# A chunk's convolutions mixed tile by tile with the projection of the chunk in front, in one buffer whose layout alternates

## The chip, the cores and the metric

One core of a Trainium2 chip. The metric is the device time of one execution in microseconds, as the median of several runs.

## The reference

The input x is (128 batch, 128 time, 512 features), float32. Two blocks are added to it, one after the other. The first is a causal convolution along time with 128 taps for each feature, two projections, and a gated linear recurrence; the second is a tanh recurrence. Cut to what matters:

```python
# block 1: conv_w = cond[:, None, :], K = 128 taps, one filter for each feature
x_pad = jnp.pad(x, ((0, 0), (K - 1, 0), (0, 0)))
conv = conv_b + sum(x_pad[:, k:k + L, :] * conv_w[k, 0] for k in range(K))
proj = conv @ Wp + bp                          # 512 -> 128
B_t, C_t = softplus(proj[..., :64]), tanh(proj[..., 64:])
u = x @ Ws + bs                                # 512 -> 64
state = decay * state + dt * B_t * u_t         # over time, y_t = C_t * state
x = x + (y @ Wo + bo)
# block 2: 128 rows, 128 steps, h0 = cond
h = tanh(h @ Wh + x_t @ Wx + b)                # over time
x = x + h
```

## The kernel before

**First phase: convolution and projection.** The 512 features are four chunks (`KC` = 4) of 128. For each feature `d` the convolution over time is one matmul, `x_ring` (time x batch, time reversed) as stationary and `t_ring`, the Toeplitz matrix of the feature's taps, as moving operand: 128 batch rows by 128 times. The float32 matmul is carried out as two records in the profile. Four features (`PER_BANK`) fill a PSUM bank; that is a tile, and a chunk has 32 (`BANKS`). Both operands come from a ring of 8 slots, each of 8 features (`CH`), 896 KB in three transfers, that SP's queue issues when `conv_done` says that the slot has been used (`load_ring`). ScalarE copies even banks and VectorE odd banks into `conv`, laid out [batch, time, feature], so each copy writes runs of four elements 512 bytes apart.

`projection(c)` starts when the chunk is copied whole. Tile m of it takes four times: four transposes turn `conv[:, t]` (batch x feature) into feature x batch in a bank of `TURN`, ScalarE copies it with the convolution's bias added to one of four slots of `turned` (`copy_turned`), and one matmul with 512 columns multiplies by the chunk's `wp_now` (two records again). Its result is added by VectorE to `bc` (`add_proj`), the sum over chunks. TensorE issues the projection of tile m - 3 after the transposes of tile m (`LAG` = 3). So TensorE's order is convolution(0), projection(0), convolution(1), and so on, the first three chunks in a loop run by the engines (`Fori`), the fourth written out. The chunk's Wp (128 x 257, with the bias as last column) is loaded by SP when the projection before has ended, behind the eight ring loads that the chunk before lets out, and ahead of the next.

**In the last chunk's projection** ScalarE and VectorE also compute the softplus of the B rows by pairs of tiles (`soft_abs`, `soft_exp`, `soft_ln`, `soft_sum`), and GpSimd splits the weights and the first x of the second phase into high and low parts, once `conv_done` says that the convolutions are over and, for `x_lo`, `turn_done` that the transposes are.

**Second phase.** 32 groups of four time steps: the recurrence of block 1 on VectorE, one group ahead of the tanh recurrence of block 2 whose products are on TensorE. It isn't touched.

Of the kernel before, what the change touches and what calls it, by code (L numbers as in the profile page):

```python
# [12 lines left out]
TIME = 128  # L13
# [11 lines left out]
VECTORS = KC + 5  # L25
PAIRS = BANKS // 2
LAG = 3
# [10 lines left out]
def build(nc, x_rev, x_dtb, hankel, h0_t, vectors, Wp, Ws, Wo, Wx, Wh, b, out):  # L38
# [6 lines left out]
    with ctx:  # L45
# [7 lines left out]
        CONV, TURN, PROJ = bank[0:4], bank[4:6] + bank[0:2], bank[2:4] + bank[6:8]  # L53
# [11 lines left out]
        wo_f = turned[:, 3]  # L65
        vec = sb(ctx, "vec", [P, VECTORS])
        bo_c, bp_c, bs_c, logs = vec[:, 0:KC], vec[:, KC:KC + 2], vec[0:N, KC + 2:KC + 3], vec[:, KC + 3:KC + 5]
        rates = sb(ctx, "rates", [P, 4])
# [6 lines left out]
        with ExitStack() as first:  # L75


            t_ring = sb(first, "t_ring", [P, RING, CH // 2, TIME, 2])
            x_ring = sb(first, "x_ring", [P, RING, CH, BATCH])
            conv = sb(first, "conv", [P, TIME, P])  # L80
# [38 lines left out]
        def f(ap):  # L119
            return ap.bitcast(F32)  # L120

# [75 lines left out]
        def _(sp):  # L197
            def load_wp(c):
                rows = bass.ds(c * P, P)
                sp.dma_start(wp_now[:], Wp[rows, :]).then_inc(wp_loaded, DMA)  # L200

# [23 lines left out]
            for q in range(per_chunk - RING):  # L225
                sp.wait_ge(conv_done, BANKS * (KC - 1) + CH // PER_BANK * (q + 1))
                load_ring(per_chunk * (KC - 1) + q + RING, q % RING)
# [115 lines left out]
        def _(act):  # L343
# [7 lines left out]
            def copy_conv(c):  # L351
                with act.Fori(0, BANKS // 4) as i:
                    m = 4 * i
                    for k in (0, 2):

                        act.wait_ge(conv_done, BANKS * c + m + k + 1)
                        nc.scalar.copy(conv[:, :, bass.ds((m + k) * PER_BANK, PER_BANK)],
                                       CONV[k][:].rearrange("p (d l) -> p l d", d=PER_BANK)).then_inc(conv_copied_act, 1)

                act.wait_ge(wp_loaded, DMA * (c + 1))  # L360

            def copy_turned(c, m, k):

                act.wait_ge(turn_done, BANKS * c + m + k + 1)
                nc.scalar.activation(turned[:, k], TURN[k][:], ACT.Identity, bias=wp_now[:, 2 * P:2 * P + 1])\
                  .then_inc(turn_copied, 1)

            act.wait_ge(weights_ready, 2)
            with act.Fori(0, KC - 1) as c:
                copy_conv(c)  # L370
                with act.Fori(0, BANKS // 4) as i:
                    for k in range(4):
                        copy_turned(c, 4 * i, k)


            nc.scalar.preload_act_table_set("natural_log_exp_and_others")
            copy_conv(KC - 1)
# [25 lines left out]
            def pair(q, i, soft_too):  # L403

                m = 2 * q - (2 * i) % 4
                copy_turned(KC - 1, m, (2 * i) % 4)
                if soft_too:
                    soft_exp(q - 3, soft[(i - 3) % SOFT_SLOTS])
                copy_turned(KC - 1, m, (2 * i) % 4 + 1)
                if soft_too:  # L410
                    soft_ln(q - 3, soft[(i - 3) % SOFT_SLOTS])
                    soft_abs_odd(q - 2, soft[(i - 2) % SOFT_SLOTS])

            for q in range(3):
                pair(q, q, False)
            soft_abs_odd(0, soft[0])
            pair(3, 3, True)
            with act.Fori(1, PAIRS // 4) as j:
                for i in range(4):
                    pair(4 * j + i, i, True)  # L420
# [50 lines left out]
        def _(dve):  # L471
# [19 lines left out]
            def copy_conv(c):  # L491
                with dve.Fori(0, BANKS // 4) as i:
                    m = 4 * i
                    for k in (1, 3):
                        dve.wait_ge(conv_done, BANKS * c + m + k + 1)
                        nc.vector.tensor_copy(conv[:, :, bass.ds((m + k) * PER_BANK, PER_BANK)],
                                              CONV[k][:].rearrange("p (d l) -> p l d", d=PER_BANK))\
                          .then_inc(conv_copied_dve, 1)

            def add_proj(c, m, k):  # L500
                dve.wait_ge(proj_done, BANKS * c + m + k + 1)
                cols = bass.ds((m + k) * 512, 512)
                nc.vector.tensor_tensor(bc[:, cols], PROJ[k][:], bc[:, cols], ALU.add).then_inc(proj_added, 1)  # L503


            copy_conv(0)
            with dve.Fori(0, BANKS // 4) as i:
                for k in range(4):
                    dve.wait_ge(proj_done, 4 * i + k + 1)
                    nc.vector.tensor_scalar(bc[:, bass.ds((4 * i + k) * 512, 512)], PROJ[k][:],  # L510
                                            bp_c[:, k % 2:k % 2 + 1], None, ALU.add).then_inc(proj_added, 1)
            with dve.Fori(1, KC - 1) as c:
                copy_conv(c)
                with dve.Fori(0, BANKS // 4) as i:
                    for k in range(4):
                        add_proj(c, 4 * i, k)


            copy_conv(KC - 1)
# [15 lines left out]
            def pair(q, i, soft_too):  # L535

                for par in range(2):
                    add_proj(KC - 1, 2 * q - (2 * i) % 4, (2 * i) % 4 + par)
                    if par == 0:
                        soft_abs_even(q, soft[i])  # L540
                    if soft_too:
                        soft_sum(q - 2, par, soft[(i - 2) % SOFT_SLOTS])

            for q in range(4):
                pair(q, q, q >= 2)
            with dve.Fori(1, PAIRS // 4) as j:
                for i in range(4):
                    pair(4 * j + i, i, True)
# [88 lines left out]
        def _(pe):  # L637
            pe.wait_ge(ident_ready, 1)

            def convolution(c):  # L640

                for d in range(P):
                    slot, m = (d // CH) % RING, d // PER_BANK
                    if d % CH == 0:
                        pe.wait_ge(t_zero, slot + 1)
                        pe.wait_ge(ring_loaded[slot], LOAD * (P // CH // RING) * c + LOAD * (d // CH // RING + 1))
# [8 lines left out]
                    if d % PER_BANK == PER_BANK - 1:  # L658
                        mm.then_inc(conv_done, 1)
# [161 lines left out]
```

## Time and profile before

| | us |
|---|---|
| median of 3 runs | 1268.31 (1265.29 to 1274.13) |
| profiled execution, its own time | 1267.0 |
| its span | 1265.2 |
| TensorE busy (share of span) | 1186.3 (94%) |
| VectorE, ScalarE, GpSimd busy | 657.2, 504.7, 333.3 |
| granted TensorE clock, mean | 0.981 |

The span runs from the first to the last instruction of the profiled execution. In the rows PE is TensorE's matmuls, PEld its weight loads, DVE VectorE, ACT ScalarE, POOL GpSimd, SPq SyncE's queue. Matmuls overlap in the records, so the pace of a row of them is read from their starts or from the length of a group, and not from one record's duration.

### The profile page before, as it was taken

What the parts mean: (1) busy time and instruction counts of PE and PEld (TensorE: products, weight loads), DVE (VectorE), ACT (ScalarE), POOL (GpSimd) and SP (SyncE); (2) the same over time, 40 slices, a digit from 0 to 9 for tenths busy, and PEclk for the clock granted to TensorE, in tenths of its full rate; (3) what the DMA queues carried; (4) which work ended last, traced back from release to release, by engine and by line L of the source; (5) the groups of instructions that cost most, each with busy time, mean ns of one, the idle gap of its engine ahead of it and who ended that gap; (6) DMA issues with size and microseconds to landing.
All of it is one profiled execution on the core that took longest, in us unless ns stands there. A gap on an engine that the chain in (4) does not pass through costs nothing.

```text
span 1265.2 us, 17115 instructions
## 1 busy us (share of the span) xinstructions
PE 1186.3 (94%) x5888; PEld 949.2 (75%) x5888; DVE 657.2 (52%) x1022; ACT 504.7 (40%) x756; POOL 333.3 (26%) x179
## 2 busy tenths in 40 slices
PE   5589799898859999999999999999999999999997
PEld 4567758577427888888888888888888888888886
DVE  2135254443996555555554555555555555455553
ACT  1144352443674434344433444443434443334432
POOL 1000000000432443333343333344333344333330
PEclk9889999998889999999999999999999999999999
DMA  9993957938102223222223322222322222322201
GB/s 213 236 233 80 271 147 205 264 96 214 45 0 67 68 81 106 80 66 66 66 66 101 98 66 66 66 66 90 101 74 66 66 66 70 107 88 66 66 34 67
DMA packets 82485, 129.54 MB, mean 102 GB/s; under 512 B 4960, under 2 KB 40800, under 8 KB 82464
## 3 DMA queue, kind: packets, MB, share of 16 engines
q1 hardware_dynamic: 82464, 129.26, 37.1%
q8 instruction: 13, 0.21, 0.1%
q14 instruction: 8, 0.07, 0.0%
HBM read 95.69 MB, written 33.55 MB: 102 GB/s over the span
## 4 chain that ended last, share of the span: by engine, by line
PE 85%; SPq 5%; DVE 3%; DMA 3%; issue 2%; ACT 0%; POOL 0%; DVEq 0%; POOLq 0%; ACTq 0%
PE bank L725 9%; PE bank L733 9%; PE bank L734 9%; PE bank L737 9%; PE bank L719 9%; PE bank L718 9%; PE bank L677 7%; PE bank L656 5%; PE bank L761 4%; PE bank L669 4%; DMA x_ring<-x_rev 3%; SPq L204 3%; PE bank L708 2%; PE bank L700 2%; PE bank L694 2%
## 5 line engine op out<-in xcount | busy, mean ns | idle before, releaser
L324 POOL TENSOR_TENSOR x_lo<-x_f,x_hi 128x512 fp32r<-128x512 f32 x126 | 160.0, 1300 | 555.7 <-ACT x_hi L442 555.7
L453 ACT ACTIVATE h_f<-z_f 128x512 f32<-128x512 f32 x128 | 80.9, 632 | 346.5 <-DVE z_f L612 346.5
L616 DVE TENSOR_TENSOR hT_lo<-bank,hT_hi 128x512 fp32r<-128x512 f32 x128 | 88.6, 692 | 216.1 <-ACT hT_hi L457 216.1
L733 PE MATMUL bank<-wh_hi,hT_hi 128*128 128x512 f32 x512 | 200.4, 391 | 0.0
L734 PE MATMUL bank<-wh_lo,hT_hi 128*128 128x512 f32 x512 | 199.8, 390 | 0.0
L719 PE MATMUL bank<-wx_lo,x_hi 128*128 128x512 f32 x512 | 199.7, 390 | 0.0
L718 PE MATMUL bank<-wx_hi,x_hi 128*128 128x512 f32 x512 | 199.4, 389 | 0.1
L656 PE MATMUL bank<-t_ring,x_ring 128*128 128x128 f32 x1024 | 134.8, 291 | 46.2 <-DMA x_ring<-x_rev 36.9
L656 PEld LDWEIGHTS bank<-t_ring,x_ring 128*128 128x128 f32 x1024 | 128.6, 202 | 53.4 <-issue 40.7
L612 DVE TENSOR_TENSOR z_f<-bank,b_rows 128x512 f32<-128x512 f32 x128 | 88.5, 692 | 132.5 <-PE bank L737 128.7
L318 POOL TENSOR_TENSOR x_lo<-x_f,x_hi 128x2048 fp32r<-128x2048 f32 x32 | 147.6, 4614 | 21.9 <-PE bank L669 21.8
L725 PE MATMUL bank<-wx_hi,x_lo 128*128 128x512 f32 x512 | 144.7, 404 | 0.3 <-POOL x_lo L324 0.3
L677 PE MATMUL bank<-turned,wp_now 128*128 128x512 f32 x256 | 133.5, 611 | 11.0 <-DVE bc L503 10.2
L737 PE MATMUL bank<-wh_hi,hT_lo 128*128 128x512 f32 x512 | 137.0, 389 | 0.0
L733 PEld LDWEIGHTS bank<-wh_hi,hT_hi 128*128 128x128 f32 x512 | 96.1, 188 | 25.9 <-ACT hT_hi L457 6.1
L457 ACT CAST hT_hi<-bank 128x512 fp32r<-128x512 f32 x128 | 75.2, 587 | 94.6 <-PE bank L761 94.6
L718 PEld LDWEIGHTS bank<-wx_hi,x_hi 128*128 128x128 f32 x512 | 96.1, 188 | 20.8 <-ACT x_hi L442 0.9
L669 PEld LDWEIGHTS bank<-ident,conv 128*128 128x128 f32 x512 | 63.3, 141 | 64.4 <-issue 64.4
L737 PEld LDWEIGHTS bank<-wh_hi,hT_lo 128*128 128x128 f32 x512 | 96.1, 188 | 20.4
L719 PEld LDWEIGHTS bank<-wx_lo,x_hi 128*128 128x128 f32 x512 | 96.1, 188 | 19.8
L734 PEld LDWEIGHTS bank<-wh_lo,hT_hi 128*128 128x128 f32 x512 | 96.2, 188 | 19.4
L442 ACT CAST x_hi<-x_f 128x512 fp32r<-128x512 f32 x128 | 79.5, 621 | 76.8 <-DVE x_f L589 74.5
(67 smaller groups left out, 1417.1 us busy)
## 6 DMA issues: line engine op xcount, KB each, us to landing
x_ring<-x_rev SPq DMA_DIRECT2D x64, 512.0 KB, 12.4
x_f<-x_dtb SPq DMA_DIRECT2D x32, 1024.0 KB, 8.1
out<-x_f SPq DMA_DIRECT2D x31, 1024.0 KB, 5.4
t_ring<-hankel SPq DMA_DIRECT2D x64, 256.0 KB, 11.4
t_ring<-hankel SPq DMA_DIRECT2D x64, 128.0 KB, 10.8
w_f<-Wx SPq DMA_DIRECT2D x1, 1024.0 KB, 5.5
w_f<-Wh SPq DMA_DIRECT2D x1, 1024.0 KB, 5.1
out<-x_f SPq DMA_DIRECT2D x4, 256.0 KB, 2.3
```

Of the source, the lines that this page charges most:

```text
L318: nc.gpsimd.tensor_tensor(x_lo[:], x_f[:, par], f(x_hi[:]), ALU.subtract).then_inc(xlo_ready, 1)
L324: nc.gpsimd.tensor_tensor(x1_lo[:, c], x1_f[:, par, c], f(x1_hi[:, c]), ALU.subtract)\
L616: nc.vector.tensor_tensor(hT_lo[:], turned_h, f(hT_hi[:]), ALU.subtract).then_inc(htlo_ready, 1)
L656: mm = nc.tensor.matmul(CONV[m % 4][:, bass.ts(d % PER_BANK, TIME)], x_ring[:, slot, d % CH], t_ring[:, slot, d % CH // 2, :, d % 2], star ...
L669: mm = nc.tensor.transpose(TURN[m % 4][:, bass.ts(i, P)], conv[:, m * PER_BANK + i], ident[:])
L677: nc.tensor.matmul(PROJ[n % 4][:], wp_now[:, bass.ts(n % 2, P)], turned[:, n % 4], start=True, stop=True)\
L718: nc.tensor.matmul(z, x1_hi[:, k, s], wx_hi[:, k], start=(k == 0), stop=False)
L719: nc.tensor.matmul(z, x1_hi[:, k, s], wx_lo[:, k], start=False, stop=False)
L725: mm = nc.tensor.matmul(z, x1_lo[:, k, s], wx_hi[:, k], start=False, stop=stop and k == KC - 1)
L733: nc.tensor.matmul(z, hT_hi[:, k], wh_hi[:, k], start=False, stop=False)
L734: nc.tensor.matmul(z, hT_hi[:, k], wh_lo[:, k], start=False, stop=False)
L737: mm = nc.tensor.matmul(z, hT_lo[:, k], wh_hi[:, k], start=False, stop=stop and k == KC - 1)
```

## The change

TensorE's order becomes: the 32 tiles of chunk 0's convolutions; then, for chunks c = 0, 1, 2 and each tile m, the transposes of tile m of chunk c, the convolutions of tile m of chunk c + 1, and the projection of tile m - 1 of chunk c; then the transposes and projections of chunk 3 with `LAG` 2. The copy of tile m of chunk c + 1 goes into the room in `conv` that the transposes of tile m of chunk c have just read. For that the layout alternates: even chunks lie as [batch, time, feature], as before, with the copy written by single elements 512 bytes apart; odd chunks lie as [batch, feature, time], with the copy contiguous and each transpose reading its 128 elements 512 bytes apart. VectorE's copies wait for `turn_done` of the tile; ScalarE's stand behind `copy_turned` of it. While chunks mix, `CONV` has four banks, `TURN` and `PROJ` two each; in the last projection four each. `turned` has three slots. Wp is loaded once (128 x 4 x 192) on SP's queue, behind the first eight ring loads; the convolution's bias moves to `vec`. All loops of the first phase are written out, and SP's ring loads depend on `conv_done` alone.

```diff
-VECTORS = KC + 5
+VECTORS = 2 * KC + 5
+WP = 3 * N
+SLOTS = 3
-LAG = 3
+LAG = 2
...
-        CONV, TURN, PROJ = bank[0:4], bank[4:6] + bank[0:2], bank[2:4] + bank[6:8]
+        CONV = bank[0:4]
+        TURN, PROJ = bank[4:6] + bank[0:2], bank[6:8] + bank[2:4]
...
-        wp_now = sb(ctx, "wp_now", [P, 2 * P + 1])
-        turned = sb(ctx, "turned", [P, 4, 512])
+        wp = sb(ctx, "wp", [P, KC, WP])
+        turned = sb(ctx, "turned", [P, SLOTS, 512])
...
+        def conv_room(c, m):
+            if c % 2:
+                return conv[:, bass.ts(m, PER_BANK)]
+            return conv[:, :, bass.ts(m, PER_BANK)].rearrange("p l d -> p d l")
+        def conv_at(c, t):
+            return conv[:, :, t] if c % 2 else conv[:, t]
+        def turn_bank(c, m):
+            return TURN[m % 4] if c == KC - 1 else TURN[m % 2]
+        def proj_bank(c, m):
+            return PROJ[m % 4] if c == KC - 1 else PROJ[m % 2]
+        def turned_slot(c, m):
+            return turned[:, (BANKS * c + m) % SLOTS]
...
@@ SP @@
-            load_wp(0)
-            per_chunk = P // CH
-            with sp.Fori(0, KC - 1) as c:
-                for q in range(per_chunk):
-                    sp.wait_ge(conv_done, BANKS * c + CH // PER_BANK * (q + 1))
-                    load_ring(per_chunk * c + q + RING, q % RING)
-                    if q == per_chunk - 1:
-                        sp.wait_ge(proj_done, BANKS * (c + 1))
-                        load_wp(c + 1)
...
+            sp.dma_start(wp[:], Wp.rearrange("(c p) n -> p c n", p=P)).then_inc(wp_loaded, DMA)
+            for n in range(RING, D // CH):
+                sp.wait_ge(conv_done, CH // PER_BANK * (n - RING + 1))
+                load_ring(n, n % RING)
@@ ScalarE @@
+            def copy_conv(c, m):
+                act.wait_ge(conv_done, BANKS * c + m + 1)
+                nc.scalar.copy(conv_room(c, m), CONV[m % 4][:].rearrange("p (d l) -> p d l", d=PER_BANK))\
+                  .then_inc(conv_copied_act, 1)
...
+            for m in range(0, BANKS, 2):
+                copy_conv(0, m)
+            for c in range(KC - 1):
+                for m in range(BANKS):
+                    copy_turned(c, m)
+                    if m % 2 == 0:
+                        copy_conv(c + 1, m)
...
@@ VectorE @@
+            def copy_conv(c, m):
+                dve.wait_ge(conv_done, BANKS * c + m + 1)
+                if c > 0:
+                    dve.wait_ge(turn_done, BANKS * (c - 1) + m + 1)
+                nc.vector.tensor_copy(conv_room(c, m), CONV[m % 4][:].rearrange("p (d l) -> p d l", d=PER_BANK))\
+                  .then_inc(conv_copied_dve, 1)
...
+            for m in range(1, BANKS, 2):
+                copy_conv(0, m)
+            for c in range(KC - 1):
+                for m in range(BANKS):
+                    if m % 2:
+                        copy_conv(c + 1, m)
+                    if m > 0:
+                        add_proj(c, m - 1)
+                add_proj(c, BANKS - 1)
@@ TensorE @@
+            def turn(c, m):
+                if m == 0:
+                    pe.wait_ge(conv_copied_act, BANKS // 2 * (c + 1))
+                    pe.wait_ge(conv_copied_dve, BANKS // 2 * (c + 1))
+                for i in range(PER_BANK):
+                    mm = nc.tensor.transpose(turn_bank(c, m)[:, bass.ts(i, P)], conv_at(c, m * PER_BANK + i), ident[:])
+                mm.then_inc(turn_done, 1)
+            def project(c, n):
+                pe.wait_ge(turn_copied, BANKS * c + n + 1)
+                freed = n - 3 if c == KC - 1 and n >= 2 else n - 1
+                wait(pe, proj_added, BANKS * c + freed)
+                nc.tensor.matmul(proj_bank(c, n)[:], wp[:, c, n % 2 * N:n % 2 * N + P], turned_slot(c, n), start=True, stop=True)\
+                  .then_inc(proj_done, 1)
+            for m in range(BANKS):
+                convolution(0, m)
+            pe.wait_ge(wp_loaded, DMA)
+            for c in range(KC - 1):
+                for m in range(BANKS):
+                    turn(c, m)
+                    convolution(c + 1, m)
+                    if m > 0:
+                        project(c, m - 1)
+                project(c, BANKS - 1)
+            for m in range(BANKS + LAG):
+                if m < BANKS:
+                    turn(KC - 1, m)
+                if m >= LAG:
+                    project(KC - 1, m - LAG)
```

## Rows read from the trace of the kernel before

**Rows 1.** Windows by stage: PE, PEld, DVE, ACT, POOL busy; PEclk, DMA share, GB/s.

```profile
8.00:75.00 67.00, 41.80 (x256) 38.28 (x256) 12.55 (x22) 9.69 (x18) 2.95 (x4) 0.87 1.09 235
75.00:117.00 42.00, 41.85 (x195) 25.06 (x196) 23.32 (x33) 21.67 (x32) 0.00 (x0) 1.00 0.62 132
117.00:153.00 36.00, 29.99 (x256) 29.03 (x254) 11.51 (x17) 9.38 (x16) 0.00 (x0) 1.00 0.98 243
...
271.00:309.00 38.00, 32.37 (x255) 31.14 (x253) 11.51 (x17) 9.38 (x16) 0.00 (x0) 0.91 0.85 197
...
382.00:1265.20 883.20, 876.44 (x4088) 718.59 (x4088) 473.04 (x764) 348.56 (x508) 301.78 (x157) 1.00 0.23 75
```

**Rows 2.** Chain that ended last: start us, us, what.

```profile
74.20 0.95 issue
75.14 1.94 PE bank L669 x16
...
308.39 0.95 issue
309.33 1.94 PE bank L669 x16
```

**Rows 3.** Timeline of TensorE in the convolutions: start us, us, what.

```profile
58.61 2.08 PE L656 MATMUL bank<-t_ring,x_ring 128*128 128x128 f32 x16 [1.90 <-DMA x_ring<-x_rev]
62.53 2.08 PE L656 MATMUL bank<-t_ring,x_ring 128*128 128x128 f32 x16 [1.85 <-DMA x_ring<-x_rev]
...
116.69 21.99 PE L656 MATMUL bank<-t_ring,x_ring 128*128 128x128 f32 x192
139.91 2.08 PE L656 MATMUL bank<-t_ring,x_ring 128*128 128x128 f32 x16 [1.23 <-DMA x_ring<-x_rev]
...
295.04 2.65 PE L656 MATMUL bank<-t_ring,x_ring 128*128 128x128 f32 x16 [2.18 <-issue]
299.33 3.75 PE L656 MATMUL bank<-t_ring,x_ring 128*128 128x128 f32 x16 [1.63 <-issue]
```

**Rows 4.** Timeline of one tile of chunk 0's projection.

```profile
79.08 0.60 PE L669 MATMUL bank<-ident,conv 128*128 128x128 f32 x4
...
79.52 1.02 PE L677 MATMUL bank<-turned,wp_now 128*128 128x512 f32 x2
...
80.38 0.60 PE L669 MATMUL bank<-ident,conv 128*128 128x128 f32 x4
80.38 0.36 PEld L669 LDWEIGHTS bank<-ident,conv 128*128 128x128 f32 x3 [0.29 <-issue]
```

**Rows 5.** DMA issues: KB each, median us from issue to landing.

```profile
x_ring<-x_rev SPq DMA_DIRECT2D x64, 512.0 KB, 12.4
...
wp_now<-Wp SPq DMA_DIRECT2D x4, 128.5 KB, 2.1
```

**Rows 6.** Groups of instructions by line, 0 to 440 us: busy, mean ns.

```profile
L365 ACT ACTIVATE turned<-bank,wp_now 128x512 f32<-128x512 f32 x128 | 86.6, 687 | 59.1 <-PE bank L669 58.7
...
L503 DVE TENSOR_TENSOR bc<-bank,bc 128x512 f32 (+1 forms) x96 | 66.1, 689 | 45.9 <-PE bank L677 45.5
L669 PEld LDWEIGHTS bank<-ident,conv 128*128 128x128 f32 x512 | 63.3, 141 | 64.4 <-issue 64.4
L496 DVE COPY conv<-bank 128x512 f32 x64 | 44.1, 691 | 121.8 <-PE bank L656 121.8
...
L357 ACT COPY conv<-bank 128x512 f32 x64 | 37.4, 586 | 135.1 <-PE bank L656 130.0 <-POOL wo_lo L279 5.1
```

**Rows 7.** Timeline of chunk 3's projection: VectorE and GpSimd.

```profile
342.16 0.69 DVE L503 TENSOR_TENSOR bc<-bank,bc 128x512 f32 x1
...
345.25 0.69 DVE L503 TENSOR_TENSOR bc<-bank,bc 128x512 f32 x1
...
358.65 4.51 POOL L318 TENSOR_TENSOR x_lo<-x_f,x_hi 128x2048 fp32r<-128x2048 f32 x1 [21.82 <-PE bank L669]
358.71 4.99 DVE L532 SCALAR_TENSOR_TENSOR bc<-bc,x_f 64x512 f32 x1
```

More of the change, by code:

```diff
@@ L79, in build @@
             x_ring = sb(first, "x_ring", [P, RING, CH, BATCH])
-            conv = sb(first, "conv", [P, TIME, P])
+            conv = sb(first, "conv", [P, P, P])
         wx_hi = sb(ctx, "wx_hi", [P, KC, D], F32R)
@@ L349, in _, with copy_turned @@
             nc.scalar.activation(rates[:, 2:4], rates_e[:], ACT.Ln, bias=1.0).then_inc(rate_act, 1)
[L351 to L365, printed above, removed]
+            def copy_conv(c, m):
+                act.wait_ge(conv_done, BANKS * c + m + 1)
+                nc.scalar.copy(conv_room(c, m), CONV[m % 4][:].rearrange("p (d l) -> p d l", d=PER_BANK))\
+                  .then_inc(conv_copied_act, 1)
+            def copy_turned(c, m):
+                act.wait_ge(turn_done, BANKS * c + m + 1)
+                nc.scalar.activation(turned_slot(c, m), turn_bank(c, m)[:], ACT.Identity, bias=conv_b[:, c:c + 1])\
                   .then_inc(turn_copied, 1)
+            act.wait_ge(vec_loaded, DMA)
             act.wait_ge(weights_ready, 2)
[L369 to L373, printed above, removed]
+            for m in range(0, BANKS, 2):
[5 more added lines that the diff above has]
+                        copy_conv(c + 1, m)
             nc.scalar.preload_act_table_set("natural_log_exp_and_others")
-            copy_conv(KC - 1)
             def u_copy(g):
@@ L401, in soft_ln @@
                 nc.scalar.activation(slot, slot, ACT.Ln, bias=1.0).then_inc(ln_ready, 1)
[L403 to L420, printed above, removed]
+            for q in range(PAIRS):
+                copy_turned(KC - 1, 2 * q)
+                if q > 2:
+                    soft_exp(q - 3, soft[(q - 3) % SOFT_SLOTS])
+                copy_turned(KC - 1, 2 * q + 1)
+                if q > 2:
+                    soft_ln(q - 3, soft[(q - 3) % SOFT_SLOTS])
+                if q > 1:
+                    soft_abs_odd(q - 2, soft[(q - 2) % SOFT_SLOTS])
             for q in range(PAIRS - 3, PAIRS):
@@ L489, in _ @@
             decay = rates[N:P, 1:2]
[L491 to L511, printed above, removed]
@@ L533, in soft_sum @@
                   .then_inc(b_ready, 1)
-            def pair(q, i, soft_too):
+            for q in range(PAIRS):
                 for par in range(2):
-                    add_proj(KC - 1, 2 * q - (2 * i) % 4, (2 * i) % 4 + par)
+                    add_proj(KC - 1, 2 * q + par)
                     if par == 0:
[L540 to L548, printed above, removed]
+                        soft_abs_even(q, soft[q % SOFT_SLOTS])
+                    if q > 1:
+                        soft_sum(q - 2, par, soft[(q - 2) % SOFT_SLOTS])
             def u_to_v(g, par):
@@ L680, in _ @@
-            with pe.Fori(0, KC - 1) as c:
-                convolution(c)
-                projection(c)
-                pe.wait_ge(proj_added, BANKS * (c + 1) - 2)
-            convolution(KC - 1)
-            projection(KC - 1)
+                mm.then_inc(conv_done, 1)
+            def turn(c, m):
[5 more added lines that the diff above has]
+                mm.then_inc(turn_done, 1)
```

58 lines of the change are left out of this document (20 added, 38 removed).

## The prediction

> **What bounds the kernel now.** I read the busy time by stage first [rows 1]. Chunk 0's convolutions (8 to 75 us) are bound by the loads: TensorE works 41.8 of 67 us while the DMA share is 1.09, all 16 queues' engines full. In each projection stage (75 to 117 us stands for three) it is the other way: TensorE is busy 41.85 of 42 us, and the DMA engines move 132 GB/s at a share of 0.62, since no more can be loaded than the ring's eight slots hold. Then the convolutions of the next chunk (117 to 153 us) find eight ready slots and sixteen to eat, and TensorE is at 29.99 of 36 us with the DMA share back at 0.98. So TensorE and the DMA engines take turns being idle. From 382 us on TensorE is busy 99% at a clock of 1.00; nothing of that recurrence is edited, and I take it as a fixed tail.
>
> Second, the chain of waits gives the borders [rows 2]: the first transpose of chunk 0 starts at 75.14 us, that of chunk 3 at 309.33. Before each lies 0.95 us in which the engine waited for nothing shown; it is the copy of the last bank (0.69 us on VectorE) that `projection` waits for. Third, the timeline of TensorE inside the convolutions [rows 3]: 192 records run in one piece (21.99 us), then pieces of 16 records (eight values of `d`, one ring slot) come singly, each released by a load. That is a used-up ring. Where the loads alone set the pace it is 62.53 - 58.61 = 3.92 us a slot in chunk 0, and at its slowest late in chunk 3, 299.33 - 295.04 = 4.29 us (named "issue", but it is the same rhythm at the same place, the thirteenth slot).
>
> **The change, part by part.** (1) *TensorE's work of the three mixed chunks.* It is the same work as before, so I price it at full pace. One tile of the projection stage repeats every 80.38 - 79.08 = 1.30 us [rows 4]: four transposes (79.08 to 79.52, 0.44 us) and two records of projection (0.86 us), with no gap. Over a stage, 41.7 us for 32 tiles (the stage's window shows 41.85 busy) is 1.303 us. The convolutions of one tile are eight records; the unbroken piece gives 21.99 us for 192, less 0.16 us of the last record's modelled drain (it lasts 0.27 us where the pace is 0.11), so 0.114 us a record and 0.91 us a tile. A mixed tile is therefore 1.30 + 0.91 = 2.21 us, and 3 x 32 of them are 212 us. Before, the same stretch took 309.33 - 75.14 = 234.2 us [rows 2]. The difference is 22.2 us. As a cross-check, it is 3 x 0.95 us of copy tails plus what the three convolution stages are longer than 29.1 us each; of 36 us in the window of chunk 1 TensorE idled 6, and chunk 3 lost more, to a clock of 0.91 as well as to waiting [rows 1].
>
> (2) *The ring.* Loads now run through the projections. A slot is eaten every two tiles, 4.42 us, against 3.92 us to fill one under full load and 4.29 us at the slowest [rows 3], so the ring gains on TensorE and the wait goes. The margin is thin at the start: chunk 0 ends with an empty ring, its last slots each being waited for, and a hiccup there shows. From the landing time of 12.4 us [rows 5] a late slot costs a part of one slot's time; I take 1 us, between 0 and 4.3 us (one whole slot at the slowest pace).
>
> (3) *Waits that the mixing adds,* all in tile m. `turn(m)` feeds the copy to `turned`, 0.69 us on ScalarE [rows 6], while TensorE has 0.91 us of convolutions and `project(m-1)` needs only the copy of the tile before, an age of 2.2 us. `project(m-1)` also needs `add_proj(m-3)`, which VectorE can begin when `project(m-3)` ends, over 3 us earlier. VectorE does per two tiles one conv copy and two adds, 3 x 0.69 = 2.07 us, ScalarE two copies to `turned` and one conv copy, 2 x 0.69 + 0.59 = 1.97 us, both of 4.42 us. VectorE's new wait on `turn_done` is met before `conv_done` of the same m, since TensorE does them in that order. ScalarE's copy of `conv(c+1, m)` blocks `copy_turned(m+1)` behind it, but that one's transposes come a full `project` later. The copy tail between chunks (0.95 us) now lies under two projections, 1.72 us. Cost 0, up to 0.05 us a tile (5 us) if the switches between three kinds of work leave bubbles that the present switches between two don't.
>
> (4) *Wp in one load.* It goes to SP's queue at the same place, behind the first eight slots and ahead of the ninth, and is 384 KB in place of 128.5 KB. Chunk 0 is bound by loads, so the 256 KB more count: at 235 GB/s [rows 1] 1.1 us. The small load takes 2.1 us to land [rows 5], so 0.5 to 3 us. The three later Wp loads, which stood in front of ring loads, go; they were hidden.
>
> (5) *The layout that alternates.* Even chunks are now copied by elements written 512 bytes apart, odd ones contiguously; the transposes of odd chunks read their weights 512 bytes apart. Before, copies wrote runs of four elements 512 bytes apart, and took 0.69 us on VectorE, the same as the contiguous add, and read their bank with that stride too [rows 6]. No row has single elements written or weights read so. For the copies I take no change (a gain is excluded, since they already take what a contiguous add of that size takes); doubled, VectorE would need 2.8 us of 4.42 and they would still be hidden. A transpose lasts 0.44 / 4 = 0.11 us, with the next weight load just under it (three loads in 0.36 us [rows 4]), so nothing hides a slower load. I take 0 here, since the bank-side stride cost nothing; the other value is a rival below.
>
> (6) *The last projection.* It is bound by VectorE: from one add of a pair to that of the next pair is 345.25 - 342.16 = 3.09 us [rows 7], against 2.6 us of TensorE for two tiles. LAG 2 in place of 3 lets the first projection start one tile's transposes earlier, 0.44 us, and takes a tile from the lead; in the steady state a projection waits for an add four back either way, and the copy needed is one pair old. `turned` with three slots is refilled only after TensorE has passed that projection. I take -0.3 us, between -1 and +3. GpSimd's splits that hold VectorE (4.99 us beside 4.51 us at 358.7 us [rows 7]) hang on the end of all convolutions and transposes, so they move along with the stage. Loops written out instead of run by the engines' counters change instruction supply; the stretch of chunk 0 runs written-out code at the loads' pace and the turn of the loop shows no gap after 116.69 us [rows 3], so 0.
>
> Sum: -22.2 + 1.0 + 1.1 - 0.3 = -20.4 us. The profiled execution took 1267.0 us (span 1265.2 and 1.8 around it), which becomes 1246.6. The median of the runs is 1.3 us above the profiled one: 1248 us. What is late next is TensorE itself through the mixed chunks, VectorE in the last projection.
>
> **A rule against the change.** The rows show strides without a price on VectorE's copies, and nothing on TensorE's weight side [rows 6]. The Trainium skill, SBUF — State Buffer, section Specifications (TRN2), says that SBUF is read by lines of 16 bytes and needs at least two hits on a line for full bandwidth. By that rule the strided weight loads of chunks 1 and 3 would slow down and the sum would be that of rival A or B; the old copies, with four elements to a line, don't contradict it.
>
> **The rivals.** *A: strided weight loads take twice their time.* A transpose then has 0.22 us; three of four loads are exposed (the first lies under a projection), 0.33 us a tile. Chunk 1: 32 x 0.33 = 10.6 us. Chunk 3: the tile becomes 1.63 us against VectorE's 1.55, 32 x 0.08 = 2.6 us. The gain of 20.4 shrinks to 7.2: 1261 us. For it: single elements in a line, and the pace of loads has no slack. Against: VectorE and ScalarE read and write at this stride at one element a cycle already [rows 6].
>
> *B, the slower side: strided weight loads take four times theirs.* Then 0.44 us each, 0.99 us more a tile: chunk 1 32 us, chunk 3 32 x (1.30 + 0.99 - 1.55) = 24 us, together 56 - 20.4 = 35 us slower, 1304 us. It costs more than the change gives from about 2.4 times on (1.4 x 0.11 x 3 = 0.46 us a tile, 15 us in chunk 1 and 7 us in chunk 3). No row shows such a price, and none excludes it.
>
> *C: the loads don't keep up.* If a slot took 4.9 us in the mix (the engines' own traffic beside it, 25% over chunk 0's 3.92), 48 slots would cost 0.48 us each, 23 us: the change only moves the wait, 1271 us. Against: the fill is 0.5 us faster than the use, and in chunk 1 the loads ran at 243 GB/s beside a busy TensorE [rows 1], where the mix asks for 0.92 MB in 4.42 us, 208 GB/s.
>
> *D: the mix leaves bubbles*, 0.05 us a tile and the ring starting empty: 1248 + 5 + 3 = 1256 us, just inside 1%.
>
> **How the numbers follow.** The forecast, the strides free and the ring ahead, 0.62; A 0.14; B 0.07; C 0.06; D 0.11. A measurement of this kernel tells no change from one within about 1%, 12.7 us. Faster by more is the forecast alone with part of D, 0.66; within 1% is A, C and the rest of D, 0.25; slower is B and the worst of C, 0.09. The forecast's own range is 1242 to 1254 (its bounds: 0 to 4.3 us for the ring, 0.5 to 3 for Wp, the last stage -1 to 3, and the runs before spread 1265.3 to 1274.1). To hold 8 in 10 it must take in D and A: 1241 to 1262.
>
> **What the profile would show.** In the mixed stretch TensorE busy at 99% with clock 1.00, a tile each 2.21 us, and DMA share about 0.85 throughout. The first transpose of chunk 3 near 288 us. No waits of the convolutions for `x_ring` after chunk 0. The last stage still 3.09 us a pair. If A or B holds, weight loads of transposes in chunks 1 and 3 last longer than the 141 ns of today's [rows 6] and those of chunks 0 and 2 don't; if C holds, waits for `x_ring` return every second tile; in D idle shows as small pieces between kinds of work. Wrong by a lot it would be if transposes read at a stride are slow, or if ScalarE's or VectorE's written strides push a copy beyond the 2.21 us of its tile.

## The result and the profile after

The changed kernel takes 1238.99 us (median of 4 runs, 1233.53 to 1241.46) against 1266.8 us before; the ratio on record is 0.9752, 95% interval 0.9711 to 0.9793 (the quotient of the two medians alone is 0.978). That is 27.8 us less by the medians, and 28.7 by the profiled executions (spans 1265.2 and 1236.5). The forecast was 1248 with a range down to 1241: right in direction, too small by 9 us.

Busy time by stage of the changed kernel, as [rows 1]: PE, PEld, DVE, ACT, POOL, then clock, DMA share and GB/s. The lines are chunk 0's convolutions, the three mixed chunks, and the fixed tail.

```profile
8.00:63.90 55.90, 35.85 (x254) 33.42 (x252) 17.87 (x22) 16.89 (x18) 2.95 (x4) 0.94 1.09 277
64.00:135.60 71.60, 71.02 (x448) 53.78 (x448) 34.20 (x47) 31.28 (x48) 0.00 (x0) 1.00 1.09 241
135.70:209.90 74.20, 74.20 (x449) 59.85 (x448) 35.91 (x49) 38.20 (x48) 0.00 (x0) 1.00 0.88 229
210.00:280.50 70.50, 70.50 (x449) 53.76 (x448) 33.09 (x48) 32.56 (x49) 0.00 (x0) 1.00 0.41 119
...
353.00:1236.50 883.50, 877.09 (x4088) 719.50 (x4088) 472.88 (x763) 348.57 (x508) 301.93 (x157) 1.00 0.24 75
```

The mix is what was forecast: TensorE is busy 71.02 of 71.6, 74.20 of 74.2 and 70.50 of 70.5 us, at a clock of 1.00. In the second chunk TensorE is as busy as in the others and the stage is 3.6 us longer: it does the same work more slowly. And chunk 0 is over at 63.9 us, with 277 GB/s where [rows 1] had 235.

The timeline of TensorE at the end of chunk 0, as [rows 3], and into the mix:

```profile
53.91 2.06 PE L639 MATMUL bank<-t_ring,x_ring 128*128 128x128 f32 x16 [1.34 <-issue]
57.30 2.05 PE L639 MATMUL bank<-t_ring,x_ring 128*128 128x128 f32 x16 [1.34 <-issue]
60.63 2.06 PE L639 MATMUL bank<-t_ring,x_ring 128*128 128x128 f32 x16 [1.28 <-issue]
63.89 0.63 PE L649 MATMUL bank<-ident,conv 128*128 128x128 f32 x4 [1.20 <-DVE conv L490]
64.82 1.18 PE L639 MATMUL bank<-t_ring,x_ring 128*128 128x128 f32 x8 [0.31 <-DMA x_ring<-x_rev]
...
68.92 1.18 PE L639 MATMUL bank<-t_ring,x_ring 128*128 128x128 f32 x8 [0.28 <-DMA x_ring<-x_rev]
...
75.21 0.60 PE L649 MATMUL bank<-ident,conv 128*128 128x128 f32 x4
...
77.41 0.60 PE L649 MATMUL bank<-ident,conv 128*128 128x128 f32 x4
```

A slot now comes every 3.4 us (53.91, 57.30, 60.63), not every 3.92 [rows 3]. The first transpose is at 63.89 us, not 75.14. Two ring waits in the mix (0.31 and 0.28 us) and then none.

The borders of the mixed chunks, where two projections follow each other (timeline of TensorE):

```profile
133.93 1.88 PE L657 MATMUL bank<-turned,wp 128*128 128x512 f32 x4
135.65 0.71 PE L649 MATMUL bank<-ident,conv 128*128 128x128 f32 x4
...
139.47 0.71 PE L649 MATMUL bank<-ident,conv 128*128 128x128 f32 x4
...
141.79 0.72 PE L649 MATMUL bank<-ident,conv 128*128 128x128 f32 x4
...
208.23 1.88 PE L657 MATMUL bank<-turned,wp 128*128 128x512 f32 x4
209.94 0.60 PE L649 MATMUL bank<-ident,conv 128*128 128x128 f32 x4
...
278.84 1.88 PE L657 MATMUL bank<-turned,wp 128*128 128x512 f32 x4
280.56 1.89 PE L649 MATMUL bank<-ident,conv 128*128 128x128 f32 x12
```

| stage | before, us | after, us | difference | forecast |
|---|---|---|---|---|
| to the first transpose | 75.14 | 63.89 | -11.25 | +1.1 |
| to chunk 3's first transpose | 234.19 | 280.56 - 63.89 = 216.67 | -17.5 | -21.2 |
| to the first `wo_product` (at 382.16 and 352.98) | 72.83 | 72.42 | -0.4 | -0.3 |
| rest | 883.04 | 883.52 | +0.5 | 0 |

The mixed stretch is 71.76 us (to 135.65), 74.29 (to 209.94) and 70.62 us. Thirty-two tiles of 2.21 us are 70.7, so the third is the sum of the forecast exactly, the first has 1.1 us of ring waits and start, and the second is 3.6 us over.

The kernel before differs much more between two profiles than the changed one. In a second profile of it (e9 below) the stretch from the first transpose to chunk 3's is 314.36 - 73.49 = 240.9 us, not 234.2; in a second profile of the changed kernel (e8) it is 276.92 - 61.37 = 215.6, not 216.7. So the second row of the table is -17.5 us in this pair of profiles and -25.3 in the other.

### The profile page after: what moved, and what is told of

It is laid out like the page before. It is cut to its first block, busy times and chain, and to the rows that moved or that the text cites. A ratio compares the mean times of both kernels' runs of the same rounds, so it can differ in the third digit from the quotient of the medians.

```text
span 1236.5 us, 15777 instructions
## 1 busy us (share of the span) xinstructions
PE 1184.0 (96%) x5888; PEld 956.6 (77%) x5888; DVE 665.2 (54%) x1022; ACT 520.5 (42%) x756; POOL 334.1 (27%) x179
## 4 chain that ended last, share of the span: by engine, by line
PE 90%; DVE 4%; DMA 2%; ACT 1%; SPq 1%; issue 1%; POOL 1%; POOLq 0%; DVEq 0%; ACTq 0%
PE bank L713 10%; PE bank L721 9%; PE bank L722 9%; PE bank L707 9%; PE bank L706 9%; PE bank L725 9%; PE bank L639 8%; PE bank L657 7%; PE bank L749 5%; PE bank L649 4%; PE bank L696 2%; PE bank L697 2%; PE bank L688 2%; PE bank L682 2%; DVE x_f L516 1%; DMA x_ring<-x_rev 1%
## 5 line engine op out<-in xcount | busy, mean ns | idle before, releaser
L639 PE MATMUL bank<-t_ring,x_ring 128*128 128x128 f32 x1024 | 140.4, 282 | 26.3 <-issue 14.3
L657 PE MATMUL bank<-turned,wp 128*128 128x512 f32 x256 | 133.7, 606 | 9.4 <-DVE bc L500 8.7
L369 ACT ACTIVATE turned<-bank,vec 128x512 f32<-128x512 f32 x128 | 87.9, 688 | 107.4 <-PE bank L649 107.1
L649 PEld LDWEIGHTS bank<-ident,conv 128*128 128x128 f32 x512 | 79.1, 190 | 62.3 <-issue 62.3
L452 ACT CAST hT_hi<-bank 128x512 fp32r<-128x512 f32 x128 | 75.1, 587 | 94.7 <-PE bank L749 94.7
```

The costliest lines, as they stand in the source:

```text
L639: mm = nc.tensor.matmul(CONV[m % 4][:, bass.ts(d % PER_BANK, TIME)], x_ring[:, slot, d % CH], t_ring[:, slot, d % CH // 2, :, d % 2], star ...
L649: mm = nc.tensor.transpose(turn_bank(c, m)[:, bass.ts(i, P)], conv_at(c, m * PER_BANK + i), ident[:])
L657: nc.tensor.matmul(proj_bank(c, n)[:], wp[:, c, n % 2 * N:n % 2 * N + P], turned_slot(c, n), start=True, stop=True)\
```

## The experiments

Chunk 0 has sixteen ring loads; I call them slot 0 to slot 15. In all experiments the "pace" is the time from TensorE's start on slot 11 to its start on slot 15, divided by four, and "first transpose" stands for the end of chunk 0. In the timeline of TensorE of the kernel before, slots 8, 11 and 15:

```profile
42.75 2.97 PE L656 MATMUL bank<-t_ring,x_ring 128*128 128x128 f32 x16 [4.01 <-DMA x_ring<-x_rev]
...
54.63 2.08 PE L656 MATMUL bank<-t_ring,x_ring 128*128 128x128 f32 x16 [1.76 <-DMA x_ring<-x_rev]
...
70.42 3.77 PE L656 MATMUL bank<-t_ring,x_ring 128*128 128x128 f32 x16 [1.05 <-DMA x_ring<-x_rev]
```

That is a pace of (70.42 - 54.63) / 4 = 3.95 us. The last slot's records took 3.77 us here, at a granted clock of 0.50 (1.2 GHz) from 70.42 to 74.20 us, and 2.06 us in the changed kernel: 1.7 of the 11.25 us are this, and not the loads.

Besides the mixing, two things differ that bear on the loads of chunk 0. `wp_now` (1028 bytes a partition, rounded up) and `turned` changed size, so all that is allocated after them moved: `t_ring` starts at byte 98080 of the partition before (32 above a multiple of 256) and at 98048 (a multiple of 256) after, `x_ring` the same. And SP's ring loads are written out. (The loops of the other engines are written out too, and Wp is one load; e6, e7 and e10 bear on these.)

**e1: the ring on the boundary, nothing else.** Two small tiles become one, which moves everything behind 32 bytes down.

```diff
-        rates = sb(ctx, "rates", [P, 4])
-        rates_e = sb(ctx, "rates_e", [P, 2])
+        rates_both = sb(ctx, "rates_both", [P, 6])
+        rates, rates_e = rates_both[:, 0:4], rates_both[:, 4:6]
...
```

> The kernel before with the ring, and all that lies behind it in SBUF, 32 bytes lower, on a multiple of 256 bytes as the change happens to put it; nothing else. Theory 'placement' (loads into rows off that boundary are slower): a ring slot fills in 3.4 us instead of 3.9, the first transpose starts near 64 us instead of 75, the convolution stages of chunks 1 to 3 shrink towards 30 us each, in all 15 to 24 us less: 1243 to 1252. Theories 'written-out loads' and 'Wp': no change, 1267.

1258.3 us, ratio 0.9885 (0.9819 to 0.9951). Slots 11 and 15 of chunk 0 in its timeline:

```profile
51.22 2.08 PE L656 MATMUL bank<-t_ring,x_ring 128*128 128x128 f32 x16 [1.14 <-DMA x_ring<-x_rev]
...
65.15 2.08 PE L656 MATMUL bank<-t_ring,x_ring 128*128 128x128 f32 x16 [1.45 <-DMA x_ring<-x_rev]
```

The pace is 3.48 us, the first transpose at 68.18. The later convolution stages didn't shrink: from the first transpose to chunk 3's it takes 301.05 - 68.18 = 232.9 us, before 234.2. So the placement speeds up the loads of chunk 0, and the first transpose comes 7 us sooner than in the first profile of the kernel before and 5.3 sooner than in the second; that it also shortens the other three stages was expected, and the profile doesn't show it. From slot 8 (41.01 us) to slot 15 it takes 24.1 us instead of 27.7.

**e2: the changed kernel, off the boundary.**

```diff
+        ring_shift = sb(ctx, "ring_shift", [P, 8])
```

> The changed kernel with 32 bytes of nothing ahead of the ring, so that it lies as before the change, off the multiple of 256 bytes. Theory 'placement': chunk 0 takes 11 us longer again, the slots of the mix are filled in 3.9 us and still in time for 4.4, so 1239 + 11 = 1250, which is about the forecast. Theories 'written-out loads' and 'Wp': 1239.

1242.49 us, ratio 0.9778 (0.9714 to 0.9842).

```profile
48.77 2.06 PE L641 MATMUL bank<-t_ring,x_ring 128*128 128x128 f32 x16 [1.63 <-issue]
...
62.81 2.05 PE L641 MATMUL bank<-t_ring,x_ring 128*128 128x128 f32 x16 [1.31 <-issue]
```

Pace 3.51 us, first transpose 66.06 against 63.89. The placement costs here, but 2 to 5 us (against 63.89 and the 61.37 of e8) and not 11: it isn't the whole. The time is 1242.5 and not the 1250 expected.

**e3: the loads written out, nothing else.**

```diff
-            with sp.Fori(0, KC - 1) as c:
+            for c in range(KC - 1):
```

> The kernel before with only SP's loop of ring loads written out, each with its own Wp as before. Theory 'written-out loads' (registers and the loop slow SP's issue): chunk 0 ends 11 us sooner, 1256 or less. Theory 'placement': the gaps between issues shrink but the queue is full anyway, 1267, first transpose at 75 us.

1266.3 us, ratio 0.9955 (0.9909 to 1.0002), first transpose 67.66, pace 3.73 us. The profile shows a gain in chunk 0, the times one that is just inside the noise. Neither theory alone was right. The gain isn't one of pace: from slot 8 (37.13 us) to slot 15 it takes 27.5 us, before 27.7. Slot 8 starts 5.6 us sooner, and the last slot runs at full clock, 1.7 us. The stretch from the first transpose to chunk 3's is 305.20 - 67.66 = 237.5 us, longer than the 234.2 of before, which eats 3.3 us of the gain.

**e4: strided weights in all chunks of the kernel before.**

```diff
-                        nc.scalar.copy(conv[:, :, bass.ds((m + k) * PER_BANK, PER_BANK)],
-                                       CONV[k][:].rearrange("p (d l) -> p l d", d=PER_BANK))
+                        nc.scalar.copy(conv[:, bass.ds((m + k) * PER_BANK, PER_BANK)],
+                                       CONV[k][:].rearrange("p (d l) -> p d l", d=PER_BANK))
...
-    nc.tensor.transpose(TURN[m % 4][:, bass.ts(i, P)], conv[:, m * PER_BANK + i], ident[:])
+    nc.tensor.transpose(TURN[m % 4][:, bass.ts(i, P)], conv[:, :, m * PER_BANK + i], ident[:])
```

(VectorE's copy alike.)

> The kernel before with the layout of odd chunks in all four: copies contiguous, every transpose reads its weights 512 bytes apart. If strided weight loads cost the 0.11 us a tile seen in the changed kernel's chunk 1 and nothing hides it: chunks 0 to 2 each 3.6 us longer, chunk 3 (bound by VectorE) not, +11 us: 1278. If the longer tile of chunk 1 came from something else in the mix (the copies' slow writes beside it): 1267, tiles of 1.30 us.

1283.82 us, ratio 1.0113 (1.0066 to 1.016). One tile in its timeline, beside [rows 4], and its groups by line, beside [rows 6]:

```profile
90.37 0.71 PE L669 MATMUL bank<-ident,conv 128*128 128x128 f32 x4
90.37 0.52 PEld L669 LDWEIGHTS bank<-ident,conv 128*128 128x128 f32 x3 [0.21 <-issue]
...
90.92 1.02 PE L677 MATMUL bank<-turned,wp_now 128*128 128x512 f32 x2
...
91.78 0.71 PE L669 MATMUL bank<-ident,conv 128*128 128x128 f32 x4
```

```profile
L669 PEld LDWEIGHTS bank<-ident,conv 128*128 128x128 f32 x512 | 92.8, 242 | 55.2 <-issue 55.2
...
L496 DVE COPY conv<-bank 128x512 f32 x64 | 44.2, 691 | 123.8 <-PE bank L656 123.8
...
L357 ACT COPY conv<-bank 128x512 f32 x64 | 37.4, 586 | 138.0 <-PE bank L656 132.9 <-POOL wo_lo L279 5.1
```

A tile repeats every 91.78 - 90.37 = 1.41 us instead of 1.30; three weight loads take 0.52 us instead of 0.36, and one 242 ns on average instead of 141, while the contiguous copies keep their 691 and 586 ns. The three projection stages are 45.5 us each instead of 41.7, 11.4 us together. From chunk 3's first transpose to the end it takes 1280.0 - 323.37 = 956.6 us, before 955.9: there VectorE hides it. What was expected of the stages held; the time, by the ratio 14 us longer, is some 3 us more than the 11 expected.

**e5: both side effects, no mixing.** The edits of e1 and e3 together.

> The kernel before with both of the changed kernel's side effects and no mixing: the ring on a multiple of 256 bytes, and SP's ring loads written out. If the two explain chunk 0 between them, the first transpose is at 64 to 65 us as in the changed kernel, and the time is about 1254 to 1256; what then still separates it from the changed kernel, some 16 us, is the mixing. If the mixing or the single Wp load speeds up chunk 0, the first transpose stays at 67 us or later.

1256.22 us, ratio 0.9896 (0.9863 to 0.993).

```profile
47.04 2.08 PE L656 MATMUL bank<-t_ring,x_ring 128*128 128x128 f32 x16 [0.86 <-DMA x_ring<-x_rev]
...
60.09 2.08 PE L656 MATMUL bank<-t_ring,x_ring 128*128 128x128 f32 x16 [1.13 <-DMA x_ring<-x_rev]
```

Pace 3.26 us, first transpose at 63.11, as in the changed kernel. From there to chunk 3's first transpose it is 297.13 - 63.11 = 234.0 us, as before (234.2). So without any mixing these two give the whole gain of chunk 0 and nothing else, and the mixing gives 234.0 - 216.7 = 17.3 us on top.

**e7: the mixing alone.** The changed kernel with e2's 32 bytes and SP's loop of before.

```diff
-            for n in range(RING, D // CH):
-                sp.wait_ge(conv_done, CH // PER_BANK * (n - RING + 1))
-                load_ring(n, n % RING)
+            with sp.Fori(0, KC - 1) as c:
+                for q in range(per_chunk):
+                    sp.wait_ge(conv_done, BANKS * c + CH // PER_BANK * (q + 1))
+                    load_ring(per_chunk * c + q + RING, q % RING)
+            for q in range(per_chunk - RING):
+                sp.wait_ge(conv_done, BANKS * (KC - 1) + CH // PER_BANK * (q + 1))
+                load_ring(per_chunk * (KC - 1) + q + RING, q % RING)
```

> The changed kernel with both side effects undone: 32 bytes ahead of the ring, and SP's loads in the loop of before. The mixing alone. If the forecast's sum was right but for these two, the first transpose is at 75 us or a little later, the mix takes 215 us, and the time is 1250, about 19 us under the kernel before. If the mixing itself is worth more than forecast: 1240.

1245.4 us (1242.15 to 1250.1), ratio 0.9809 (0.9761 to 0.9857), which on 1268.3 is 1244 (1238 to 1250); the forecast of 1248 lies in it. Pace 3.62 us. But the first transpose was expected at 75 us or a little later, and is at 68.37. Slot 8 begins at 38.05 us, where the kernel before has 42.75 and 42.62, though the ring and the loop are the same. So undoing the two side effects gives back only part of chunk 0: 5 to 7 us of its gain remain, and no run says by what. The mixed stretch is 284.51 - 68.37 = 216.1 us. By the profiles' spans the kernel is 24.7 us shorter than before, 6.8 of them in chunk 0 and 18.1 in the stretch: that its time agrees with the forecast is in part luck, since the forecast had chunk 0 longer and the mix worth more.

**e6: Wp later.** The one Wp load goes behind ring load 16 instead of 7 (counted from 0).

> The changed kernel with Wp's one load issued behind ring load 16 and not behind the eighth. If it takes its bytes' share of chunk 0 (384 KB at the 277 GB/s there, 1.4 us), the first transpose comes 1.4 us sooner and the time falls by about 1 us, within the noise of the times but not of the profile. If small rows of 768 bytes cost more: 2 to 3 us. If the queue hides it: nothing.

1240.13 us, ratio 0.9767 (0.9721 to 0.9812), pace 3.39 us.

```profile
61.10 2.05 PE L640 MATMUL bank<-t_ring,x_ring 128*128 128x128 f32 x16 [1.25 <-issue]
66.09 0.66 PE L650 MATMUL bank<-ident,conv 128*128 128x128 f32 x4 [2.94 <-DMA wp<-Wp]
```

The first transpose is later than with Wp early (63.89 and 61.37 in two profiles), because it now waits for Wp itself: the load was moved so far back that TensorE stands idle for 2.94 us before the mix, where the changed kernel has 1.20. What the loads of chunk 0 gain is therefore read from slot 15, at 61.10 us with Wp behind its loads, against 60.63 and 58.12 us with Wp ahead of them. No gain of the size expected; Wp's price in chunk 0 is below what one profile can tell, and may be nothing.

**e8 and e9: the two kernels again,** for how far profiles of one kernel differ.

> The changed kernel itself, on the chip and beside the runs of these three, for a second profile: how far do the stages differ between two profiles of one kernel. Expected 1239, first transpose within 1 us of 63.9, mixed stages of 71.8, 74.3 and 70.6 us within 0.5.

1238.07 us, ratio 0.9744 (0.9697 to 0.9791). First transpose 61.37, 2.5 us sooner and not within 1 us, pace 3.24 us.

```profile
61.37 0.63 PE L649 MATMUL bank<-ident,conv 128*128 128x128 f32 x4 [1.20 <-DVE conv L490]
...
276.92 1.89 PE L649 MATMUL bank<-ident,conv 128*128 128x128 f32 x12
```

The mixed stages, with borders at 132.00 and 206.31 us, are 70.6, 74.3 and 70.6 us: the last two as in the first profile, the first 1.1 us shorter, as no ring wait is left in it.

> The kernel before itself, for a second profile of it. So far three kernels with the loads in SP's loop and TensorE's, ScalarE's and VectorE's loops too begin slot 8 at 41.0 to 43.7 us, and the rest at 35.4 to 38.1. If that is the kernel and not the execution: slot 8 at 41 to 44 us here again, then 3.9 us a slot, first transpose at 74 to 76. If it is the execution: anything between.

One run of 1271.7 us.

```profile
54.58 2.08 PE L656 MATMUL bank<-t_ring,x_ring 128*128 128x128 f32 x16 [1.82 <-DMA x_ring<-x_rev]
...
70.47 2.08 PE L656 MATMUL bank<-t_ring,x_ring 128*128 128x128 f32 x16 [1.75 <-DMA x_ring<-x_rev]
73.49 1.94 PE L669 MATMUL bank<-ident,conv 128*128 128x128 f32 x16 [0.95 <-issue]
...
314.36 1.94 PE L669 MATMUL bank<-ident,conv 128*128 128x128 f32 x16 [0.95 <-issue]
```

First transpose at 73.49, a little sooner than the 74 to 76 us expected, since the last slot ran at full clock this time (2.08 us for 3.77); pace 3.97 us, slot 8 at 42.62. So chunk 0 varies by 1.7 and 2.5 us between two profiles of a kernel, and what separates the kernels (75.1 and 73.5 against 63.9 and 61.4) is about four times that.

The stretch to chunk 3's first transpose varies more in the kernel before: 234.2 and 240.9 us here, 232.9, 234.0 and 237.5 in e1, e5 and e3, which share its order of work. The three projections in it take the same in all five; the convolution stages, where TensorE waits for loads (and loses some clock in `before`, e3 and e9), are 34.2 to 41.3. In the eight profiles with the mixed order it is 215.5 to 216.7. So the mixing is worth 16 to 25 us, and the 17.3 us above are one pair's.

**e10: Wp inside the loop,** chunk by chunk, on top of e7.

```diff
-            sp.dma_start(wp[:], Wp.rearrange("(c p) n -> p c n", p=P)).then_inc(wp_loaded, DMA)
+            sp.dma_start(wp[:, 0], Wp[0:P, :]).then_inc(wp_loaded, DMA)
...
+                sp.dma_start(wp[:, bass.ds(c + 1, 1)], Wp[bass.ds((c + 1) * P, P), :]).then_inc(wp_loaded, DMA)
```

> The changed kernel, ring shifted by 32 bytes and loads looped as in e7, and now each chunk's Wp loaded by itself, the later three at the end of the loop's body as before the change. If the Wp load in SP's loop is what delays the start: slot 8 at 41 to 44 us and first transpose near 74. If not (the loops of the other engines, or none of these): slot 8 near 38 us and first transpose near 68, as e7.

One run of 1241.11 us. Pace 3.92 us, slot 8 at 37.06, first transpose at 67.68. The Wp load in the loop doesn't delay the start, and a second kernel with the ring and the loop of before has its first transpose at 68 and not at 74.

**e11 and e12: 64 and 128 bytes** ahead of the changed kernel's ring.

> The changed kernel with 64 bytes ahead of the ring. If every start off a multiple of 256 bytes costs: a slot fills in 3.6 us late in chunk 0, as with 32 bytes. If a multiple of 64 is enough: 3.2 to 3.4 us, as the changed kernel.

> The changed kernel with 128 bytes ahead of the ring: by the same two readings 3.6 us a slot, or 3.2 to 3.4.

Single runs of 1244.31 and 1241.62 us. Slots 11 and 15 of e11, then of e12:

```profile
52.75 2.06 PE L641 MATMUL bank<-t_ring,x_ring 128*128 128x128 f32 x16 [1.55 <-issue]
...
66.95 2.06 PE L641 MATMUL bank<-t_ring,x_ring 128*128 128x128 f32 x16 [1.42 <-issue]
```

```profile
49.24 2.05 PE L641 MATMUL bank<-t_ring,x_ring 128*128 128x128 f32 x16 [1.55 <-issue]
...
63.26 2.06 PE L641 MATMUL bank<-t_ring,x_ring 128*128 128x128 f32 x16 [1.34 <-issue]
```

First transposes at 70.20 and 66.51 us. 3.55 and 3.51 us a slot, as with 32 bytes (3.51): by these single profiles a multiple of 64 or 128 is not enough. All paces side by side:

| us a slot | off the multiple of 256 | on it |
|---|---|---|
| loads in SP's loop | 3.95, 3.97 (before), 4.14 (e4), 3.92 (e10), 3.62 (e7) | 3.48 (e1) |
| loads written out | 3.73 (e3), 3.51 (e2), 3.55 (e11), 3.51 (e12) | 3.38, 3.24 (after), 3.26 (e5), 3.39 (e6) |

The two columns don't overlap; the two rows do on the left. The placement is what shows in the pace.

## Why the prediction was wrong

**What failed is the term for chunk 0**, +1.1 us in step (4), and with it the premise of steps (1) and (4) that the loads of chunk 0 keep the pace that the trace of before shows. I looked for what the change does to the bytes that are loaded, and not for where they go or how they are issued. Measured, that term is -11.25 us, in a second pair of profiles 61.37 - 73.49 = -12.1. Two side effects are enough for it without any mixing: where the ring lies and that the loads are written out. e5 has both and no mixing, and the same chunk 0 (63.11 us). Alone they give 7.0 us (e1) and 7.5 us (e3), together 12.0, each read to the 2 us by which two profiles of one kernel differ. By the times, e5 is 1.04% under the kernel before, 13 us. They work at different places. From the start of slot 8 to that of slot 15 it takes 22.7 to 25.1 us with the ring on the multiple of 256 bytes (five profiles), and 25.1 to 29.0 off it (nine). Written-out loads in the kernel before move the start of slot 8 from 42.75 to 37.13 us and leave that stretch alone. But the two are not all: with both undone in the changed kernel (e7, e10) the first transpose is at 68.4 and 67.7 us and not at 75, so something else in the change can give 5 to 7.5 us of it without them. What it is stays open, and so does how much each of the two gives in the changed kernel. Of the 11.25 us, 7.0 are gained before slot 8, 2.8 from there to slot 15, and 1.5 behind it, where the slot that ran at clock 0.50 before runs at 1.00; in the second pair it is 7.2, 5.1 and -0.2.

How writing out the loads works is open as well. Its gain comes before slot 8, whose load is the first that the loop issues: in both profiles of the kernel before and in e1 and e4, the fourth slot's `x_ring` issue lasts 1.6 to 2.2 us, and slot 8 begins at 41.0 to 43.7 us. The same issue in the timeline of SP's queue of the kernel before, then of the changed one:

```profile
9.91 1.69 SPq L206 DMA_DIRECT2D x_ring<-x_rev  x1
```

```profile
9.67 0.60 SPq L225 DMA_DIRECT2D x_ring<-x_rev  x1
```

Elsewhere that issue lasts 0.60 to 0.66 us and slot 8 begins at 35.4 to 38.2, e7 and e10 with their loop among them, except e11 (1.21 us, 40.3). In the loop, SP's queue also stands idle for 0.2 to 0.3 us before each issue, written out for 0.04 to 0.05 us; again in the kernel before:

```profile
34.49 1.56 SPq L206 DMA_DIRECT2D x_ring<-x_rev  x1
36.32 2.64 SPq L204 DMA_DIRECT2D t_ring<-hankel  x2
```

e7 and e10 have these gaps too and start early all the same, so the gaps don't explain the start. Whether it is SP's program, the other engines' loops, or the moment at which queues fill, no run tells apart; that the Wp load in the loop does it is refuted by e10.

**Steps (1) and (2), the mix: right.** Tiles of 2.21 us (77.41 - 75.21 = 2.20 above), no ring wait after the first microseconds. The ring's allowance of 1 us met 1.1 us in one profile and 0 in the other. The gain was forecast as 234.2 us before less 212 after. The 212 (212.2 unrounded) stood, but for step (5); the 234.2 moves by 7 us between two profiles, and the forecast had no room for that. The DMA share, 1.09, 0.88 and 0.41 in the three chunks, is not the 0.85 throughout that I expected, because the loads ran ahead: in the first mixed chunk 19 slots are issued for 16 used, in the third only 8 are left to load.

**Step (3), the added waits: right, 0.** The third chunk's 70.62 us leave no room for bubbles; rival D fell. So did rival C: no ring wait shows after 69 us.

**Step (5), the layout: wrong, and hidden for the greater part.** The groups by line in the first mixed chunk (contiguous copies, contiguous weights), then in the second:

```profile
L649 PEld LDWEIGHTS bank<-ident,conv 128*128 128x128 f32 x128 | 15.8, 140 | 17.2 <-issue 17.2
L490 DVE COPY conv<-bank 128x512 f32<-128x512 f32 x16 | 11.4, 711 | 14.3 <-PE bank L639 14.3
L363 ACT COPY conv<-bank 128x512 f32<-128x512 f32 x16 | 9.4, 587 | 4.7 <-PE bank L639 4.7
```

```profile
L649 PEld LDWEIGHTS bank<-ident,conv 128*128 128x128 f32 x122 | 22.5, 240 | 12.9 <-issue 12.9
...
L490 DVE COPY conv<-bank 128x512 f32<-128x512 f32 x15 | 15.4, 1030 | 13.0 <-PE bank L639 13.0
L363 ACT COPY conv<-bank 128x512 f32<-128x512 f32 x15 | 15.4, 1027 | 3.4 <-PE bank L639 3.4
```

A copy by single elements 512 bytes apart takes 1.03 us on either engine, 2.0 ns an element, where runs of four took 0.69 and 0.59 [rows 6]; I had taken no change, and had read the runs of four as if the engines already wrote single elements at that stride. ScalarE and VectorE had the room. A strided weight load takes 240 ns for 140. Of that TensorE's tile feels 0.12 us (139.47 to 141.79 is 2.32 us), 3.6 us in chunk 1 and none in chunk 3. Rival A, twice the time for a load, was the right mechanism at a third of the price: I had 0.33 us a tile, because I took the load's pace as what doubles. By the rows one load goes from 140 to 240 ns and three back to back only from 0.36 to 0.52 us [rows 4, e4], so most of the added time overlaps with the next load. The rule that I weighed there, the Trainium skill's in SBUF — State Buffer, section Specifications (TRN2), that a line of 16 bytes needs at least two hits for full bandwidth, is borne out in direction by both rows, weights and copies, and by the copies with four elements to a line, which had no price.

**Step (6): right.** -0.4 for -0.3.

Without chunk 0 the steps summed to -22.2 + 1.0 - 0.3 = -21.5 us and came out at -17.4 in the pair of profiles that was forecast from: 3.6 us of the difference are step (5), 0.5 the tail, which nothing edits. In the second pair they came out at -25.1, since the kernel before took 240.9 us for its stretch. The forecast lies between, so its account of the mix is right in mechanism, and its size is shown only to these 8 us. The range was too narrow below because step (4) was bounded at 0.5 to 3 us, as a loss only, with no reason that excluded a gain.

## What to carry to other kernels

Resizing a tile moves every tile behind it, so before forecasting a change to a stage bound by loads compare the addresses too: here a move of 32 bytes changed the pace of the loads by 12% (e1) or 4% (e2). Take a second profile before an old stage's length goes into a sum: stages that wait for loads moved by 7 us here between two profiles of one kernel. When two stages each leave idle what the other is short of, the price of mixing them is read off directly: the sum of the two stages' TensorE paces per tile, here 70.7 us forecast and 70.62 found in the chunk without strides. A layout that alternates should turn its costly side to the stage with another bound, as chunk 3's strided reads, which cost nothing.

## What the runs showed of the hardware

- The loads of one slot are 512 KB in rows of 4 KB (128 partitions), 256 KB in rows of 1 KB and 128 KB in rows of 512 bytes (64 partitions, four rows each). Together they take 3.24 to 3.48 us where the ring starts on a multiple of 256 bytes of the partition, and 3.51 to 4.14 us where it starts 32, 64 or 128 bytes beside one. The Trainium skill, DMA: Bandwidth & Descriptors, section How a descriptor splits into AXI transactions, says that a descriptor is split into transactions of 256 bytes, and that one which doesn't start on a multiple of 256 bytes has its first transaction start at the multiple below. An estimate by that page: a piece of 512 bytes that starts 32 bytes above a multiple would need three transactions for two, and one of 4 KB seventeen for sixteen. The page speaks of reads and these are the writes' addresses, so the agreement is in direction only.
- Strided by 512 bytes with float32: copies on VectorE and ScalarE take 1.03 us for 512 elements a partition, for 0.69 and 0.59 us in runs of four; a weight load of 128 columns takes 240 ns for 140.
- SP's queue stands idle 0.2 to 0.3 us before each DMA issue in a loop run by its counters, and 0.04 to 0.05 us where the loads are written out (`before`, e1, e4, e7, e9 and e10 against the rest).
- The times of the kernel before scattered from 1260.6 to 1282.4 us over the runs, those of the changed one from 1233.4 to 1242.1.
